# A decoder's last norm moved into the attention heads before it, with its logits on four column strips

## The reference

```python
x = x + _L1_xattn_ref(_layernorm(x, axis=-1), ctx_1024, ...)
x = x + _L1_ffn_ref(_layernorm(x, axis=-1), L1_ffn_gate_w, L1_ffn_w1, L1_ffn_w2, L1_ffn_w3)

def _layernorm(x, axis=-1, eps=1e-05):
    m = jnp.mean(x, axis=axis, keepdims=True)
    v = jnp.var(x, axis=axis, keepdims=True)
    return (x - m) / jnp.sqrt(v + eps)

# _L1_ffn_ref: x is 2048 tokens, 12 experts, the best 2 of each token
logits = x @ gate_w.T
probs = jax.nn.softmax(logits, axis=-1)
rw, sel = jax.lax.top_k(probs, TOP_K)
```

## Time and profile before

| | us |
|---|---|
| median of three runs | 3646.77 (3645.39 to 3648.10) |
| profiled execution | 3662.09 |
| its span, first to last instruction | 3660.3 |
| busy: PE, DVE, ACT, POOL | 3219.4, 2431.8, 1773.1, 1203.4 |
| mean granted TensorE clock | 0.944 |

### The profile page before, as it was taken

How to read it: one execution, slowest core, us unless ns; L and a number is a source line. 1 busy time by engine, 2 the same in 40 slices (tenths; PEclk the granted TensorE clock), 3 DMA queues, 4 the chain that set the end, 5 groups by cost and what they waited for, 6 DMA issues and landing times. The chain is left out here.

```text
span 3660.3 us, 34737 instructions
## 1 busy us (share of the span) xinstructions
PE 3219.4 (88%) x11045; PEld 1571.0 (43%) x11045; DVE 2431.8 (66%) x4472; ACT 1773.1 (48%) x3342; POOL 1203.4 (33%) x963
## 2 busy tenths in 40 slices
PE   3750699999999799999999999899899978999963
PEld 3330244444444345555455555344444444444432
DVE  8768899999999555555555555543421266999754
ACT  4748466666666334343434343344310125888621
POOL 0323699999999001010000000021388020000024
PEclk9975799999999899999999999999999997999977
DMA  7115425353432222222211111243622011000056
GB/s 258 48 60 166 149 93 147 100 138 101 124 112 75 99 74 67 69 78 66 70 52 52 61 55 52 95 139 123 231 106 98 0 64 58 1 1 1 1 162 212
DMA packets 201318, 334.67 MB, mean 91 GB/s; under 512 B 25648, under 2 KB 76208, under 8 KB 198064
## 3 DMA queue, kind: packets, MB, share of 16 engines
q1 hardware_dynamic: 187904, 298.69, 25.0%
q0 software_dynamic: 12208, 33.57, 3.3%
q10 hardware_dynamic: 1024, 0.20, 0.0%
HBM read 217.69 MB, written 114.69 MB: 91 GB/s over the span
## 5 line engine op out<-in xcount | busy, mean ns | idle before, releaser
L1282 POOL TENSOR_TENSOR sc_dBu<-sc_dtu,xa 128x1024 f32<-128x1024 f32 x256 | 540.0, 2131 | 42.1 <-DMA sc_dtu<-scan_dtu 32.9
L1192 PE MATMUL y_ps<-sc_g,ident 128*128 128x512 f32 x1024 | 476.0, 600 | 18.5 <-POOL sc_g L1270 11.6
L1306 DVE TENSOR_TENSOR_SCAN sc_dA<-sc_dA,sc_dBu 128x1024 f32<-128x1024 f32 x160 | 365.1, 2282 | 7.1 <-POOL sc_dBu L1282 7.1
L1565 ACT ACTIVATE c_p<-c_ps,c_sm 128x512 f32<-128x512 f32 x256 | 195.6, 774 | 352.9 <-DVE c_sm L1606 352.9
L1605 DVE TENSOR_REDUCE c_sm<-c_ps 128x4 f32<-128x2048 f32 x64 | 146.7, 2292 | 313.1 <-PE c_ps L1528 313.1
L1246 ACT ACTIVATE sc_dA<-sc_dt,a_neg 128x511 f32<-128x511 f32 x512 | 329.6, 676 | 11.4 <-DVE sc_g L1306 9.8
L1192 PEld LDWEIGHTS y_ps<-sc_g,ident 128*128 128x128 f32 x1024 | 190.0, 190 | 256.1 <-issue 169.2
L1598 DVE SCALAR_TENSOR_TENSOR xa<-c_ps,c_sm,xa 128x512 f32<-128x512 f32 x256 | 192.2, 751 | 146.9 <-PE c_ps L1518 133.3
L1518 PE MATMUL c_ps<-c_wo,c_oT 128*128 128x512 f32 x512 | 246.5, 605 | 2.3 <-DVE xa L1598 1.6
L1499 PE MATMUL c_ps<-u,c_wq 128*128 128x512 f32 x512 | 231.9, 596 | 4.5 <-DMA c_wq<-in_c_wq_dram 4.5
L1547 PE MATMUL c_ps<-c_pT,c_v 128*128 128x512 f32 x512 | 231.7, 595 | 2.8 <-DVE c_pT L1617 2.8
(11 more groups left out here) (516 smaller groups left out, 6089.8 us busy)
## 6 DMA issues: line engine op xcount, KB each, us to landing
kv_w<-in_c_wkv_dram SPq DMA_DIRECT2D x32, 512.0 KB, 4.0
cross_keys<-kv_out SPq DMA_DIRECT2D x64, 256.0 KB, 2.0
cross_values<-kv_out SPq DMA_DIRECT2D x128, 128.0 KB, 1.9
c_kT<-cross_keys SPq DMA_DIRECT2D x64, 256.0 KB
c_rk<-cross_rk SPq DMA_DIRECT2D x64, 256.0 KB
c_v<-cross_values SPq DMA_DIRECT2D x64, 256.0 KB, 2.6
expert_rows<-e_yt SPq DMA_DIRECT2D x63, 256.0 KB, 2.0
xa<-scan_bc SPq DMA_DIRECT2D x48, 256.0 KB, 7.9
```

Source lines behind the costliest of these rows:

```text
L1192: ins = pe.matmul(yps[:, k % 2, :], ident[:], g[:, c % GS, n, :], start=False, stop=(m == NCH - 1 and n == NG - 1))
L1282: pool.tensor_tensor(dBu[:, c % 3], spread(dtu[:, k % DT, :], NG), bc[:, m * NG:(m + 1) * NG, :], ALU.mult).then_inc(s_dBu, 1)
L1306: dve.tensor_tensor_scan(to.rearrange("p n s -> p (n s)"), dA[:, c % 2].rearrange("p n s -> p (n s)"), dBu[:, c % 3].rearrange("p n s -> p ...
L1565: ins = act.activation(pr[:, j, :], ps[:, SB + j, :], ACT.Exp, scale=rq[:, j:j + 1], bias=bias[:, j:j + 1], accum_out=l[:, j:j + 1])
```

## The change

- `norm_all` in front of the last experts is gone. Its work is done by `Norm` inside `heads1`, whose section gets SP's list and 12 more semaphores.
- DVE measures each tile of `xa` three steps after its addition (11 tiles in the loop, from the second batch on), and takes the scales in three groups: tiles 0 to 7 at step 103, 8 to 11 behind the loop, 12 to 15 at the end.
- ACT applies tiles 0 to 7 in 16 steps of the last batch, one in every second step; 8 to 11 after it has copied four transposed tiles, and 12 to 15 behind its last copy. `xn` lies in the room of the keys, whose layout becomes one block per batch, so that the first batches' room is free.
- The rows are stored by SP from within the heads' section.
- PE transposes behind the last output product, through three banks instead of four. `qT` takes the place of `xT`.
- The logits of a batch are four products, one for each chunk, into four strips of 32 partitions of one bank, each with gate weights padded to 32 columns with zeros (a memset at the section's start; the weights' load waits for it). `pick` (three additions at the section's start) has 1 where a strip's row belongs to an expert, so that the placing product adds the four strips.
- The copy of the logits from their bank (L2742) is now the last step of the heads' section. The expert weights are loaded by SP at the start of the experts' section, and PE waits for them before its first hidden product.

```diff
 
         wo = sb("c1_wo", [P, HC, H])
         xT, second = attention_tiles(d)
-        kT = spare.rearrange("p c (b s) -> p b c s", b=NB)
+        room = spare.rearrange("p c t -> p (c t)")
+        kT = room.rearrange("p (b c s) -> p b c s", b=NB, c=HC)
+        xn = room.rearrange("p (t n) -> p t n", n=H)
         v = second.rearrange("p (b j) n -> p b j n", b=NB)
...
     oT = qT
     dc = ctx.enter_context(nc.sbuf_tensor("h1_dc", [P, RING, 2, DCA], F32))
     sm = ctx.enter_context(nc.sbuf_tensor("h1_sm", [P, RING, 4, 2, 2], F32))
+    work = ctx.enter_context(nc.sbuf_tensor("h1_nm", [P, 11 * NB * TT], F32))
+    gw = ctx.enter_context(nc.sbuf_tensor("h1_gw", [P, HC, HD], F32))
+    lgT = ctx.enter_context(nc.sbuf_tensor("h1_lgT", [P, 2, S], F32))
+    pick = ctx.enter_context(nc.sbuf_tensor("h1_pick", [P, NE1], F32))
+    NT = NB * TT
+    ACTS = NT // 2
     scale = HD ** -0.5
...
 
     with section(nc, "h1_S", "h1_bias", "h1_exp", "h1_rl", "h1_pd", "h1_T", "h1_ea", "h1_O", "h1_Oe", "h1_Y", "h1_ye",
-                 "h1_own") as (block, s_S, s_bias, s_exp, s_rl, s_pd, s_T, s_ea, s_O, s_Oe, s_Y, s_ye, s_own):
+                 "h1_own", "h1_gz", "h1_gl", "h1_pk", "nm_rs_e1", "nm_xn_e1", "nm_tr_e1", "nm_cp_e1", "nm_cd_e1", "nm_row_e1",
+                 "e1_lgT", "e1_lgk", "e1_lgp") as (
+            block, s_S, s_bias, s_exp, s_rl, s_pd, s_T, s_ea, s_O, s_Oe, s_Y, s_ye, s_own, s_gz, s_gl, s_pk, s_rs, s_xn, s_tr,
+            s_cp, s_cd, s_row, s_lg, s_lk, s_lp):
+        norm = Norm(work, (0, ACTS, NT - TT, NT), xa, qT, xn, [ps[:, k, :] for k in (PT, PT + 1, YB)], ident,
+                    (s_rs, s_xn, s_tr, s_cp))
+        gates, placed_ps = ps[:, OB, :], ps[:, 0, 0:NT * NE1]
+
+        @block.sync
+        def _(sp):
+            sp.wait_ge(s_gz, 1)
+            sp.dma_start(gw[:, :, 0:NE1], A["e1_gwT"].rearrange("(c p) e -> p c e", p=P)).then_inc(s_gl, 16)
+            for t in range(NT):
+                sp.wait_ge(s_xn, t + 1)
+                sp.dma_start(rows[t * P:(t + 1) * P, :], xn[:, t, :]).then_inc(s_row, 16)
+            sp.wait_ge(s_gl, 16)
+            sp.wait_ge(s_row, 16 * NT)
+
         @block.tensor
...
+            def copied(t):
+                if t < ACTS:
+                    pe.wait_ge(s_cp, t + 1)
+                else:
+                    pe.wait_ge(s_cd, t - ACTS + 1)
+
+            def turned(t):
+                if t == 0:
+                    pe.wait_ge(s_ea, N)
+                    pe.wait_ge(s_ye, (NB - 1) * TT)
+                if t >= 3:
+                    copied(t - 3)
+                pe.wait_ge(s_xn, t + 1)
+                for c in range(HC):
+                    ins = pe.transpose(norm.banks[t % 3][:, c * P:(c + 1) * P], xn[:, t, c * P:(c + 1) * P], ident[:])
+                ins.then_inc(s_tr, 1)
+
+            def logits(b):
+                if b == 0:
+                    pe.wait_ge(s_gl, 16)
+                    pe.wait_ge(s_Oe, NB * HC)
+                else:
+                    pe.wait_ge(s_lk, b)
+                for t in range(b * TT, (b + 1) * TT):
+                    copied(t)
+                for c in range(HC):
+                    ins = pe.matmul(gates[c * HD:(c + 1) * HD, :], gw[:, c, :], qT[:, c, b * S:(b + 1) * S], start=True, stop=True)
+                ins.then_inc(s_lg, 1)
+
+            def placed(b):
+                pe.wait_ge(s_lk, b + 1)
+                if b == 0:
+                    pe.wait_ge(s_pk, 3)
+                    pe.wait_ge(s_ye, (NB - 1) * TT + 1)
+                for j in range(TT):
+                    t = b * TT + j
+                    ins = pe.matmul(placed_ps[:, t * NE1:(t + 1) * NE1], lgT[:, b % 2, j * P:(j + 1) * P], pick[:],
+                                    start=True, stop=True)
+                ins.then_inc(s_lp, 1)
+
+            for t in range(NT):
+                turned(t)
+                if t % TT == 1 and t > TT:
+                    logits(t // TT - 1)
+                if t % TT == 0 and t >= 2 * TT:
+                    placed(t // TT - 2)
+            logits(NB - 1)
+            placed(NB - 2)
+            placed(NB - 1)
+
...
                     if k and j == TT // 2 and pair == 0:
                         gathered(k - 1)
+                    if e >= N - BATCH + SET and e % 2 and e < N - BATCH + SET + 2 * ACTS:
+                        norm.applied(act, (e - (N - BATCH + SET)) // 2)
             gathered(N // SET - 1)
+            for t in range(ACTS):
+                if t == TT:
+                    for k in range(ACTS, NT - TT):
+                        norm.applied(act, k)
+                norm.copied(act, t)
+            for t in range(NT - TT, NT):
+                norm.applied(act, t)
 
         @block.vector
...
 
+            dve.memset(gw[:], 0.0).then_inc(s_gz, 1)
+            for k in range(3):
+                dve.tensor_tensor(pick[:], ident[:, 0:NE1] if k == 0 else pick[:], ident[:, (k + 1) * HD:(k + 1) * HD + NE1],
+                                  ALU.add).then_inc(s_pk, 1)
+                dve.wait_ge(s_pk, k + 1)
             for s in range(N + 2):
                 if s < N:
...
                 if s >= 2 and finished(s - 2):
                     added(*finished(s - 2), YB)
+                if s >= 5 and finished(s - 5):
+                    b, j = finished(s - 5)
+                    dve.wait_ge(s_ye, b * TT + j + 1)
+                    norm.measured(dve, own, b * TT + j)
+                if s == N - BATCH + 7:
+                    norm.scales(dve, own, 0)
             added(NB - 2, TT - 1, YB)
+            dve.wait_ge(s_ye, (NB - 1) * TT)
+            norm.measured(dve, own, (NB - 1) * TT - 1)
+            norm.scales(dve, own, 1)
             for j in range(TT):
                 added(NB - 1, j, j)
-
+                dve.wait_ge(s_ye, (NB - 1) * TT + j + 1)
+                norm.measured(dve, own, (NB - 1) * TT + j)
+            norm.scales(dve, own, 2)
+
+            def copied(t):
+                dve.wait_ge(s_tr, t + 1)
+                dve.tensor_copy(qT[:, :, t * P:(t + 1) * P],
+                                norm.banks[t % 3].rearrange("p (c t) -> p c t", c=HC)).then_inc(s_cd, 1)
+
+            def kept(b):
+                dve.wait_ge(s_lg, b + 1)
+                if b >= 2:
+                    dve.wait_ge(s_lp, b - 1)
+                dve.tensor_copy(lgT[:, b % 2, :], gates).then_inc(s_lk, 1)
+
+            kept(0)
+            for t in range(ACTS, NT):
+                copied(t)
+                if t % TT == 1:
+                    kept(t // TT - 1)
+            kept(NB - 1)
+            dve.wait_ge(s_lp, NB)
+            dve.tensor_copy(lg, placed_ps)
...
-        gw = sb("e1_gw", [P, HC, NE1])
         w13 = sb("e1_w13", [P, HC, NE1, 2 * FE])
         w2 = sb("e1_w2", [FE, NE1, H])
         lps = ctx.enter_context(nc.psum_tensor("e1_lps", [P, S], F32))
-        with ExitStack() as c2:
-            xT = c2.enter_context(nc.sbuf_tensor("e1_xT", [P, HC, T], F32))
-            norm_all(nc, "e1", xa, xT, ident, loads=[(w13[:], A["e1_w13"]), (w2[:], A["e1_w2"])],
-                     rows=rows, gate=(gw, A["e1_gwT"].rearrange("(c p) e -> p c e", p=P), lps))
...
             def _(sp):
+                sp.dma_start(w13[:], A["e1_w13"]).then_inc(s_wl, 16)
+                sp.dma_start(w2[:], A["e1_w2"]).then_inc(s_wl, 16)
+                sp.wait_ge(s_wl, 32)
                 for t in range(TL):
...
                 turned(0)
+                pe.wait_ge(s_wl, 32)
                 for e in range(NE1 + 1):
...
                 own = Order(dve, s_own)
-                own.after(dve.tensor_copy(lg[:].rearrange("p j e -> p (j e)"), lps[:, 0:NTT * NE1]))
-                own.after(dve.tensor_reduce(sm[:, 0, :], lg[:], AX_X, ALU.max))
-                dve.tensor_tensor(lg[:], lg[:], along(sm[:, 0, :], NE1), ALU.subtract).then_inc(s_cen, 1)
+                own.after(dve.tensor_reduce(sm[:, 0, :], lg, AX_X, ALU.max))
+                dve.tensor_tensor(lg, lg, along(sm[:, 0, :], NE1), ALU.subtract).then_inc(s_cen, 1)
...
-            cross1(nc, A, xa, d, spare, ident, kn, vn, kst, wqc)
-        experts1(nc, A, rows, parts, xa, out.rearrange("b (j p) c -> p (b j) c", p=P), ident, ctx)
+            cross1(nc, A, xa, d, spare, ident, kn, vn, kst, wqc, rows, lg)
+        experts1(nc, A, rows, parts, xa, out.rearrange("b (j p) c -> p (b j) c", p=P), lg, ident, ctx)
 
 
```

More of the change, by code:

```diff
@@ L2207, in _, with cross1 @@
                         added(b)
-def cross1(nc, A, xa, d, spare, ident, kn, vn, kst, wqc):
+def cross1(nc, A, xa, d, spare, ident, kn, vn, kst, wqc, rows, lg):
     with ExitStack() as ctx:
@@ L2232, in cross1 @@
         with ExitStack() as c2:
-            heads1(nc, xT, kT, v, wo, xa, ident, c2)
+            heads1(nc, A, xT, kT, v, wo, xa, xn, rows, lg, ident, c2)
 def qkv1(nc, A, wq, bq, bo, wo, aff, xT, kr, kn, vn, kst, kT, v, xa, ident, ctx):
@@ L2353, in _, with heads1 @@
                 normalise(b)
-def heads1(nc, qT, kT, v, wo, xa, ident, ctx):
```

(16 more changed lines are left out.)

## The result

| | before | after |
|---|---|---|
| median of six runs, us | 3646.67 (3645.39 to 3648.10) | 3632.18 (3628.78 to 3635.50) |
| profiled execution, its span | 3662.09, 3660.3 | 3631.06, 3629.2 |

The ratio is 0.9962, 95% interval 0.9952 to 0.9972: 14.5 us faster, where 20.9 were forecast. The two profiled executions differ by 31 us, and that is no measure of the change: in the one of before, the heads' first step on DVE stands at 3065.1 us, in the one of after at 3048.3, and nothing that differs is ahead of it. So I measure from this step, and cut the rest in three: to the start of the last of the eight passes of the last output products (heads), from there to the maximum over the logits (tail), and on to the end.

What follows compares the result with a forecast made beforehand. Bound: a serial chain of stages in the norm section before the last experts' barrier. Tail gain 22.4 less a 1.5 us heads stall gives 20.9 us, so 3625.9 us (0.57% faster); range 3622 to 3636.5.

Steps and rivals of the forecast that it cites:

- What bounds the end: Last experts' routing, gathers and products run in series behind an all-engine barrier; whatever moves the barrier moves the end.
- Statistics in the loop are free, one per set: Heads: one tile measured on DVE, 0.94 us, makes a set 23.94 of PE's 24.09 us; no cost.
- The prediction's sign of being wrong: Heads: sets in batches 1 and 2 longer than 24.2 us would speak against the forecast.
- The first group's scales cost 1.5 us: Last batch of the heads: 2.51 us of scales on DVE don't fit, so PE stalls about 1.4, taken as 1.5.
- The lag of 3.0 and the 1.6 that PE bears: Last batch: DVE lag of 0.5 plus 2.51 us of scales makes 3.0; PE bears about 1.6 before stalling.
- ACT's applied tiles, the row stores, the weights: Eight applies and row stores in the heads, expert weights loaded later, at about 3494: each priced 0.
- The tail takes 19.0 us: Last output product to first routing step shortens by 22.4 us; in the study's measure from 41.4 to 19.0.
- Prices at full clock: Tail: steps priced at full clock, such as 0.51 us for a tile's transposes, 0.48 an ACT copy, 0.71 an apply.
- the placing products stay at about 0.41: Tail: placing a batch's logits on PE keeps its old price, about 0.41 us.
- The strips: Tail: a batch's logits as four side-by-side 32-column products take 1.0 us instead of 3.6; rival of no overlap, chance 0.06.
- The rule on drains: Tail: tiling-mode changes drain PE, 1.4 us at most for four logits, half already contained; no term added.
- The clock rival: Heads: last-batch stalls cost PE its clock, 45 us against the 22.4 gained, 23 us slower, 3669.7; chance 0.03.

Runs made afterwards that it cites:

- measured twice: Changed kernel with each of the 11 tiles measured in the heads' loop measured a second time; ratio to before 0.9993.
- short scales: Changed kernel with the first group's scales cut from 13 DVE steps to two, reciprocal square root left out (result differs); ratio to before 0.9946.
- late ones: Changed kernel with scales of tiles 0 to 7 taken at the loop's end and ACT applying these tiles in one block; ratio to before 0.9945.
- shifted: Changed kernel with 13 unread transposes ahead of the last batch's output products, so the tail begins 1.7 us later; single run, 3631.10 us.
- kept warm: Changed kernel with 17 unread transposes added in PE's two waits of the tail; ratio to before 0.9935.

## Why the prediction was right or wrong

- **What bounds the end**: right. The stage behind the barrier moved as a block: 143.4 and 141.5 us before, 142.6 and 141.4 after.
- **Statistics in the loop are free, one per set**: right, to 0.01 us counted from PE's scores, and the second is not (measured twice). The prediction's sign of being wrong, a set of batches 1 and 2 over 24.2, shows once if one counts by DVE: 24.34 for the set of steps 40 to 47, in which the first tile is measured. From there DVE is 0.25 us later, and PE loses nothing by it. (The prediction took every set of the last three batches for 24.09; the first set of batch 1 takes 23.10 by PE's scores and 22.44 by DVE, before and after.)
- **The first group's scales cost 1.5 us**: 1.7. The lag of 3.0 and the 1.6 that PE bears were nearly the right pair: DVE is 0.25 + 2.50 us late at the end of that set, and PE loses 1.4 there. That the scales are the cause is shown by the short scales (1.7 back) and the late ones (1.6 back).
- **ACT's applied tiles, the row stores, the weights**: free, as said. L2815 is 31.5 us behind the first routing step in both kernels; the last weights landed 17.4 us after they were asked for, where 27.5 were allowed.
- **The tail takes 19.0 us**: it takes 24.5. Two terms were wrong. The step "Prices at full clock" failed: I foresaw a wait of about 2 us of PE on the copy of tile 4 (1.53 came) and did not ask what it does to the clock. It cost 3.7 us (shifted, kept warm). And "the placing products stay at about 0.41" took the price of a transpose for what is now a product with `pick`: two passes each, 0.96 us for a batch, four times; up to 2.2 us, which is about the 1.8 that is left between 19.0 and 20.8. In the shifted kernel's rows logits 3 end 0.9 us later than in the prediction's schedule, with two batches' placing ahead of them on PE, and the last placing ends 1.1 us behind its logits' copy instead of 0.4. That these 1.8 are the placing products alone is argued from the rows, not shown: no run has strips and short placing together.
- **The strips**: the price of 1.0 was right (1.07). Their worth in the tail was 6.3 us net of the longer placing, not the 10 of "four logits at 2.5 each": with the longer logits PE has no wait for the other engines left until before logits 3.
- **The rule on drains** (the Trainium skill, TensorEngine Tiling (Array Packing), Key Properties): from the strips at 3476.53 to the next transposes at 3477.53 in the shifted kernel's tail 1.00 us passes, no more than the strips' own 1.06; no term for it was needed.
- **The clock rival** had the right resource at the wrong place. I placed it in the heads, with a price of 45 us; there the clock stayed with PE's wait of 1.19 us, and was seen to fall only when PE waited 2.15 us (measured twice). In the tail it took 3.7.
- **The number**: the way it moved and the size of the gain were forecast, 6.4 us too much of it. The range held partly by luck: its high end was made for longer hand-overs, late weights and strips that don't overlap, none of which came, and the clock and the placing products, which it did not take in, fell into that room. They are 5.5 of the 6.4; the rest is within what two profiles of one kernel differ.

## What to carry to other kernels

Cost moved work by what the engine needs when it is behind, not by its idle time: here 23.0 of 24.09 us, and one block of 0.94 fits, two don't. When a schedule of the new order shows the matrix engine waiting even 1.5 us, price its products once at either clock level. And look for stretches in which that engine is busy and its clock is low: a few dense products gave more (10.4 us) than the rest of the tail's tuning.

## What the runs showed of the hardware

TensorE can be busy for nearly all of a stretch and still be held at 1.2 GHz: at the heads' start for 47.8 us in nine of twelve profiles and for 41.0 to 44.4 in the other three, with products of 32 rows and 128-column transposes (30.7 of 30.8 us busy in the second set of before's second profile). Four products of 128x512 behind the first scores, in one profile, had it at 2.4 GHz 2.0 us behind their start, and with one per step it stayed there. The Trainium skill, TensorE: Matmul & The Clock Gate, What's actually happening, has the clock released by activity; these rows show that busy time in the profile is not that activity. A wait of 1.5 us in the tail cost the clock for about 7 us in two profiles and not at all in four with the same instructions there.
